# Counting equal edge keys by products of key bits, with ScalarE taking three tiles of four

## The reference, cut to what matters

```
msg = relu(x[src] + edge_attr @ We + be)                 # first layer, first list
agg = segment_sum(msg, dst)
...
e = leaky_relu(a_src[src] + a_dst[dst])                  # sixth layer, second list
e_max = segment_max(e, dst); ee = exp(e - e_max[dst]); denom = segment_sum(ee, dst)
agg = segment_sum(h[src] * alpha, dst)
```

## Time and profile before

| | |
|---|---|
| median of three runs | 6771.24 us (6770.72 to 6789.09) |
| profiled execution, device time | 6782.71 us |
| its span | 6780.9 us |
| edges stage, POOL's first to last add of sums | 113.2 to 1732.2 us |
| last pair add issued | 4047.8 us |
| mean granted TensorE clock | 0.869 of full speed |

### The profile page before, as it was taken

How to read it: one execution, slowest core, us unless ns; L and a number is a source line. 1 busy time by engine, 2 the same in 40 slices (tenths; PEclk the granted TensorE clock), 3 DMA queues, 4 the chain that set the end, 5 groups by cost and what they waited for, 6 DMA issues and landing times.

```text
span 6780.9 us, 84375 instructions
## 1 busy us (share of the span) xinstructions
PE 5263.8 (78%) x25932; PEld 3305.6 (49%) x25932; DVE 3662.2 (54%) x7414; ACT 1579.7 (23%) x2506; POOL 3049.3 (45%) x2048
## 2 busy tenths in 40 slices
PE   3777767788599888987458707766698999899899
PEld 2555555556455665566346507611265333222266
DVE  5777777777411211122125307699812998767732
ACT  0111111111222102200112201355422002555421
POOL 1577777788888777877777870000000000000000
PEclk9787888888699989998778758899899999999889
DMA  7665565544655785586999659533200011222200
GB/s 161 161 123 107 114 113 109 86 64 64 51 15 16 54 94 19 11 91 60 126 110 99 36 17 185 109 107 106 81 14 15 27 30 31 72 69 73 59 16 24
DMA packets 588774, 495.10 MB, mean 73 GB/s; under 512 B 411556, under 2 KB 547925, under 8 KB 582585
## 3 DMA queue, kind: packets, MB, share of 16 engines
q1 hardware_dynamic: 294993, 401.39, 28.2%
q0 software_dynamic: 261696, 90.13, 21.8%
q10 hardware_dynamic: 31896, 1.11, 0.3%
HBM read 348.94 MB, written 143.47 MB: 73 GB/s over the span
## 4 chain that ended last, share of the span: by engine, by line
PE 24%; POOL 23%; DVE 11%; issue 9%; DMA 8%; ACT 1%; SPq 0%; DVEq 0%; ACTq 0%; POOLq 0%
POOL pairs L645 23%; DMA pairs<-PAIR_CNT,PAIR_IDX 7%; PE PS L1903 5%; PE PS L1771 5%; PE PS L912 4%; PE PS L884 4%; DVE WORK L1655 4%; DVE MXS L1812 3%; PE PS L1324 2%; PE PS L1792 1%; DVE WORK L1661 1%; DMA WORK<-pairs 1%; PE PS L1893 1%; DVE WORK L1958 1%; PE PS L1291 1%
## 5 line engine op out<-in xcount | busy, mean ns | idle before, releaser
L645 POOL DMA_INDIRECT pairs<-PAIR_CNT,PAIR_IDX x1364 | 2176.0, 1595 | 542.1 <-issue 424.0
L471 DVE SCALAR_TENSOR_TENSOR XT<-PS,ROWS,XT 128x512 f32<-128x512 f32 (+1 forms) x1364 | 938.2, 744 | 151.6 <-PE PS L463 140.8
L1002 DVE SCALAR_TENSOR_TENSOR X<-PS,G,X 125x256 f32<-125x256 f32 x520 | 227.9, 480 | 1069.3 <-PE PS L912 995.0
L1324 PE MATMUL PS<-IDENT,WORK 125*125 125x125 f32 x2400 | 336.4, 312 | 425.9 <-DMA WORK<-pairs 378.7
L685 POOL DMA_INDIRECT sums<-WORK,ROWS x340 | 529.4, 1557 | 289.7 <-issue 191.4
L1958 DVE SCALAR_TENSOR_TENSOR WORK<-WORK 125x1000 f32<-125x1000 f32 x400 | 462.2, 1197 | 203.7 <-ACT WORK L1933 203.7
L1392 DVE CUSTOM_DVE_ANT_0 ROWS<-ROWS 125x2500 f32<-125x2500 f32 x100 | 276.4, 2764 | 517.5 <-ACT ROWS L1332 503.7
L912 PE MATMUL PS<-WORK 128*125 128x256 f32 x2400 | 538.7, 379 | 8.9 <-ACT WORK L968 8.9
L1324 PEld LDWEIGHTS PS<-IDENT,WORK 125*125 125x125 f32 x2400 | 330.0, 227 | 432.3 <-issue 432.3
L884 PE MATMUL PS<-XT,WORK 128*128 128x500 f32 x1200 | 533.3, 591 | 7.5 <-DVE X L954 5.4
L912 PEld LDWEIGHTS PS<-WORK 128*125 128x125 f32 x2400 | 449.6, 188 | 129.0 <-issue 68.2
(11 more groups left out here) (272 smaller groups left out, 6871.4 us busy)
## 6 DMA issues: line engine op xcount, KB each, us to landing
WORK<-pairs SPq DMA_DIRECT2D x400, 218.8 KB
pairs<-ROWS SPq DMA_DIRECT2D x75, 976.6 KB
WORK<-pairs SPq DMA_DIRECT2D x60, 1093.8 KB
WORK<-pairs SPq DMA_DIRECT2D x80, 546.9 KB
pairs<-PAIR_CNT,PAIR_IDX POOLq DMA_INDIRECT x1364
WORK<-pairs SPq DMA_DIRECT2D x40, 382.8 KB
mask_t<-ROWS SPq DMA_DIRECT2D x20, 546.9 KB
WORK<-mask_t SPq DMA_DIRECT2D x20, 546.9 KB
```

The lines of the kernel that those rows point to most:

```text
L471: st.go(dve.scalar_tensor_tensor(KEY_JUNK[0:n, q, 0:SUPER * n], PS[0:n, bank, 0:SUPER * n], cols[0:n, q:q + 1], weights, ALU.is_equal, ALU ...
L645: pool.indirect_dma_start(table, bass.IndirectOffsetOnAxis(idx[:, n:n + 1], 0), cnt[:, n:n + 1], None, compute_op=ALU.add).then_inc(sem(do ...
L1324: ins = pe.matmul(PS[0:P, b // 4, (b % 4) * P:(b % 4 + 1) * P], flat(WORK, (2 * c + u) * N, T, P)[0:P, b, :], IDENT[0:P, 0:P], start=c == ...
```

## The change

- The codes of the second list are made in another way. SP loads each super's 512 source and 512 destination indices, both broadcast over 16 partitions (`keys`, six DMAs per group). DVE takes the minimum with the last valid value, then extracts one bit per partition by a shift and a mask, and writes bit - 0.5 in bf16 (`bits`, three instructions of 96 x 512 per group, in the group before the one that uses them). PE multiplies the 32 x 128 bits of a tile by the 32 x 512 bits of the super: the product is 8.0 exactly where all 32 bits agree (`alike`).
- For three tiles of four PE adds a second bf16 product that puts a bonus on earlier places, and ScalarE makes the code by one relu with a scale, a bias and a sum over the row (`code`). The fourth tile's code is still made by DVE, by one comparison of the product with 8.0 (`alike_codes`). The first list's codes stay as they are (`key_codes`).
- PSUM banks are shared out anew: one bank for spread destinations and one for sums in place of two each, two for the codes of ScalarE. ACT's order in a step becomes: code, code, copy of the sums of the step before, relu of the messages, code.
- The 36 parameter loads go from ACT's queue at the start of the stage to SP's queue behind the last zeroing round (after group 60). The setup loads the second list in rows of 128 indices, and the keys are transposed by PE (eight 128 x 128) at the stage's end. A few constants are added. POOL's program is unchanged.

```
+            def keys(g, u):
+                hold(sp, "keys_taken", g + 1)
+                for r in range(S2):
...
+                    for c in range(2):
+                        sp.dma_start(KEYS2[u][32 * r + 16 * c:32 * r + 16 * c + 16],
+                                     a["L2_ffn_edge_index"][c, span].partition_broadcast(16)
+                                     ).then_inc(sem(f"keys_loaded{u}"), 16)
...
+            params(sp)
+            with sp.Fori(ZI + ZP, (NG - 1) // 2 - 1) as i:
...
+        def alike(pe, u, j, q, bank, bonus):
+            bits = BITS2[u][32 * j:32 * j + 32]
+            ins = pe.matmul(PS[:, bank, :], bits[:, q * 128:(q + 1) * 128], bits, start=True, stop=not bonus)
+            if bonus:
+                n = (q + 1) * 128
+                ins = pe.matmul(PS[:, bank, 0:n], ALIKE_B, BONUS[:, (SUPER - 1) * 128 - n:], start=False, stop=True)
...
+        def alike_codes(dve, st, q, code, bank):
+            st.go(dve.scalar_tensor_tensor(KEY_JUNK[:, q, :], PS[:, bank, :], BIT_EQUAL, weights_of(BEFORE2, q),
+                                           ALU.is_equal, ALU.mult, accum_out=code))
...
         def edges_act(act):
-            params_act(act)
...
+                    hold(act, "act_rows", g * (ACT_TILES * S2) + (ACT_TILES * j + q + 1))
+                    like = PS[:, act_bank(u, j, q), :]
+                    act.activation(like, like, ACT.Relu, bias=ACT_LESS, scale=BIT_SCALE,
+                                   accum_out=CODE2[:, u, SUPER * j + q:SUPER * j + q + 1]
...
+            def bits(g, u, n=32 * S2):
+                hold(dve, f"keys_loaded{u}", keys_in(u, g))
+                st.step(dve.tensor_scalar(KEYS2[u], KEYS2[u], KEY_MOST[0:n], None, ALU.min))
+                st.step(dve.tensor_scalar(BIT2[u], KEYS2[u], BIT[0:n], 1, ALU.logical_shift_right, ALU.bitwise_and))
+                dve.sem_inc(sem("keys_taken"), 1)
+                dve.tensor_scalar(BITS2[u], BIT2[u], 0.5, None, ALU.subtract).then_inc(sem("bits_ready"), 1)
```

More of the change, by code:

```diff
@@ L22 @@
 I32 = mybir.dt.int32
+BF16 = mybir.dt.bfloat16
 ALU = mybir.AluOpType
@@ L46 @@
 SUPER = 4
+BIT_EQUAL, BIT_BONUS, BIT_SCALE = 8.0, 0.25, 4.0 * RANK
 LOCAL = 40
@@ L388, in setup_dve, with bit_consts @@
             st.step(dve.tensor_tensor(K2F, K2F, S2F, ALU.max))
+            bit_consts(dve, st)
             stage_end(dve)
+        KEY_MOST, ACT_LESS, BIT_LESS = (EDGE_C[:, c:c + 1] for c in range(3))
+        BIT = EDGE_C[:, 3:4].bitcast(I32)
+        def bit_consts(dve, st):
+            part, upper = EDGE_C[:, 4:5].bitcast(I32), EDGE_C[:, 5:6].bitcast(I32)
+            st.go(dve.memset(ACT_LESS, 1.0 - BIT_EQUAL * BIT_SCALE))
+            st.go(dve.memset(BIT_LESS, -0.5))
+            st.step(dve.tensor_scalar(part, SPARE[:, 0:1], float(N), None, ALU.subtract))
+            st.go(dve.tensor_scalar(BIT, part, 15, None, ALU.bitwise_and))
+            st.step(dve.tensor_scalar(upper, part, 4, 1, ALU.logical_shift_right, ALU.bitwise_and))
+            st.step(dve.tensor_scalar(KEY_MOST, upper, float(N - 1), None, ALU.add))
         NG = K1 // GR
@@ L427, in group @@
                 sp.dma_start(EA_T[0:ED, u, :], a["edge_t"][:, ds(g * (GR * P), GR * P)]
-                             if not isinstance(g, int) else a["edge_t"][:, 0:GR * P]).then_inc(sem(f"ea_loaded{u}"), 16)
+                             if not isinstance(g, int) else a["edge_t"][:, g * (GR * P):(g + 1) * (GR * P)]
+                             ).then_inc(sem(f"ea_loaded{u}"), 16)
+                keys(g + 1, 1 - u)
+            keys(0, 0)
             group(0, 0)
@@ L595, in group @@
                                           ).then_inc(sem("rows_coded"), 1)
+                    if j == 0:
+                        if not isinstance(g, int):
+                            hold(dve, "act_rows", g * (ACT_TILES * S2))
+                        bits(g + 1, 1 - u)
                     if j == 1:
@@ L599, in group @@
                     st.wait()
-                    keys, codes, before, n = step_keys(u, j)
-                    key_codes(dve, st, keys, codes, before, n, 6 + b)
+                    if j < S2:
+                        alike_codes(dve, st, ACT_TILES, CODE2[:, u, SUPER * j + ACT_TILES:SUPER * (j + 1)], KEY_BANK + b)
+                    else:
+                        key_codes(dve, st, COLG[:, u, GR:2 * GR], CODE_P[:, u * GR:(u + 1) * GR], P, KEY_BANK + b)
                 st.wait()
```

145 lines of the change are left out of this document (102 added, 43 removed).

## The result

The changed kernel took 7045.8 us (median of four executions, 7011.7 to 7088.0), the kernel before 6780.2 us beside it (four, 6770.7 to 6789.3): a ratio of 1.0395, 95% interval 1.0319 to 1.0471. That is 266 us slower, far past the range of 6728 to 6815. The profiled execution has a span of 7012.3 us, 231 more than before's 6780.9; it is among the faster of the four. The slower ones were granted less clock over the whole span: 7011.7 and 7014.2 us go with 0.826, 7077.4 and 7088.0 us with 0.817.

A forecast was written before the change was run, and what follows sets the result against it. POOL was taken to bound the kernel, at 18.3 us a group in the edges stage. Terms -25 + 0 + 10 + 2 + 3 + 0 = -10, from 6771.2 to 6761 us; range 6728 to 6815.

The forecast's parts named there:

- What bounds the kernel now: Edges stage: POOL is full at 18.26 us a group from 1260 us on; the codes' copies lie 14 us ahead.
- The start, -25: Start of the edges stage: PE no longer waits for ACT's parameter loads, first add of sums at 88 us, 25 us gained.
- DVE, PE and ACT in the groups, 0: Edges-stage groups: all three stay under POOL's 18.3 us, PE near 16, so cost and gain are nothing.
- a rival with a chance of 0.04: Edges-stage groups: PE becomes the bound if products cost f32 column prices, or clock stays near half; +230 to +340; chance 0.04.
- Contention, +10: SBUF in the edges stage: DVE's three bit instructions a group hold up POOL, 0.12 us a group, 10 us in all.
- The slower rival: Edges stage: DVE's bit instructions meet POOL's start or end in every group; at 0.9 us a group +57, 6828 us; chance 0.15.
- Zeroing rounds, +2: Edges stage, DMA: key loads make zeros start 3 us later against POOL's adds; +2, over 30 rounds -20 to +25.
- Parameters, +3: Behind group 60: SP is held 34 us by the parameter loads, mostly covered by PE's lead; +3, from 0 to 15.
- The tail, 0: End of the edges stage: codes, transposes and indices end some 2 us later, before POOL needs them; 0.

The follow-up runs named there:

- over 96 rows: The changed kernel with each product of bits over 96 rows instead of 32; only the edges stage read: adds end at 1709.2 us against 1965.5, 19.11 us per group.
- The loads alone: The kernel before with only its 36 parameter loads moved from ScalarE's start to SyncE behind its last group: 6764.9 us against 6788.9, ratio 0.9955.
- before with the loads at this place: The kernel before with only its 36 parameter loads moved to SyncE behind the zeroing rounds (after group 60): 6756.2 us, ratio 0.9956.
- VectorE's and ScalarE's blocks: The changed kernel, loads last, products over 96 rows, 64 of them zeros; the stationary operand's blocks written by VectorE (ratio to before 1.0013) or by ScalarE (1.0036).

## Why the prediction was wrong, by its own steps

- **What bounds the kernel now:** right. POOL sets 18.3 us a group; over 96 rows the change runs at POOL's pace again, at 18.35 us from group 60 to 71. The lead was read too large: the 14 us are those of ScalarE's copies, but the first add of a group also waits for VectorE's row indices, and these were as little as 5 us ahead. It is there that the lead ran out.
- **The start, -25:** -18.4 in the change, first add at 94.8 instead of 88. Over 96 rows it is 89.9 (-23.3). Most of the miss is PE again: from its release to the first add it took 14.5 us before, now 21.8, and 15.9 over 96 rows. The clock column reads 1.00 for these microseconds, but the instructions don't: the spread of destinations (569), 0.38 us at full clock, takes 0.63 up to the one at 92.25 us in the change, and 0.38 from 84.58 us on over 96 rows. The loads alone bring -31.
- **DVE, PE and ACT in the groups, 0:** the step that failed. PE was to need near 16 us a group, under POOL's 18.3; it needed 21.3, and the term put at nothing cost about 235 us: 127 up to group 59, 11 in groups 60 and 61, 97 behind them. The price of a bf16 column was fairly judged: over 32 rows at clock 0.80 the estimate above gives 17.4 us, and over 96 rows 15.3 are measured (467.6 of 600 us, at 19.6 us a group), where I took 16. The weight loads that aren't hidden beside 32 rows, 2.0 to 2.9 us a group, had no term. What failed is the sentence that the slower half of PE's steps would be made good in the faster: I took the clock to be PE's to keep as long as PE has no gaps, and named 21.5 to 23 us a group as a rival with a chance of 0.04. The rival came true, through its second clause, the granted clock near half. The trace of before couldn't show it, since every product there has 64 to 128 rows; that the change's have 32 stood in the diff, with its slices of 32. (ScalarE's work was also put too low, 8.5 us: a code takes 0.66 us and 0.19 more to read its sum, so it has 10.7. The run in which it reads 8 columns shows that this cost nothing.)
- **Contention, +10:** 0 as far as shown: POOL's means stayed at 1.549 and 1.567, and at 1.553 over 96 rows from 1260 to 1700 us, where POOL is full, although VectorE's three instructions last 1.56 us in place of 1.35. The slower rival's mechanism exists, but with six such instructions a group, not three: 0.2 us a group.
- **Zeroing rounds, +2:** right to within the noise (19.11 us a group over 96 rows, 19.10 before), but by luck, since two errors cancel: over 350 to 1250 us from before to 96 rows POOL's waits in front of its adds of sums shrank from 117 to 62 us, and those in front of its pair adds grew from 41 to 94.
- **Parameters, +3:** 0 where there is a lead (before with the loads at this place, and 96 rows), and with the lead gone 17 us in groups 60 and 61. The step said that the cost hangs on PE's lead, and then took the lead for granted.
- **The tail, 0:** right within 2 us.

The Trainium skill (TensorE: Matmul & The Clock Gate, Part 1) says that the clock is gated by how busy PE has been, and warns of idle gaps. The trace agrees in the stretch of before shown above, where half clock follows PE's waits. It doesn't cover this case: with PE busy all the time from 796 to 832 us, 0.50 was granted. Here the measurements decide: the rows that a product occupies count too. The Trainium skill (SBUF — State Buffer, "Who interferes with whom") says that VectorE's 2-port instructions lock POOL out while ScalarE never does; the runs with VectorE's and ScalarE's blocks agree, 1.586 against 1.554 us. With only the three instructions of 96 x 512, which the prediction counted under the same rule, POOL's mean stayed at 1.549, so no cost of theirs shows.

## What to carry to other kernels

Packing a product into fewer rows of the array isn't free even if PE has time for its columns. Ask what the clock will be, and not only how long the instruction is at the clock of today; and ask how soon the next product can start, not only how long one lasts. If a mean granted clock falls while PE has no gaps, count the rows of its products. Here adding idle products of 128 rows brought the clock back, and padding with zeros to 96 rows brought back the clock and hid the weight loads. To find what a waiting engine waits for, go by its program as well as by the nearest row: the copy that stood beside POOL's add wasn't its releaser. And when a step is costed at nothing because of another engine's lead, every other step that leans on the same lead falls with it, as the parameter loads did; the part of an edit that pays (here the loads) is worth running alone.

## What the runs showed of the hardware that was not expected

- The granted clock in one and the same loop, with PE 94 to 97% busy where it is the bound: 0.56 with products of 32 rows and no bonus products, 0.63 to 0.66 with them (nine a group, 128 rows), 0.69 and 0.86 with twelve more of 128 and 512 columns, 0.71 with products of 64 rows. With 96 rows it is 0.80 although PE is busy only 78%.
- Beside products of 32 or 64 rows the next weight load starts only at the end of the product ahead: 0.53 us from start to start at half clock and 0.32 at full, where over 96 rows it is 0.42 and 0.22, for the same 512 columns.
- With 32 rows, PE busy for 36 us without a gap (796 to 832 us) was granted half clock all the time.
- Zeros count as rows in use, both as weights (0.80 with 64 of 96 rows zero) and as moving data (0.86).
- Why before's products of 64 rows and f32 keep the clock up, and whether the type plays a part beside the rows, no run tells.
